# A cross-attention and routed FFN kernel: router scores spread by two transfers, normalised rows turned by VectorE and transfers, and the key projections moved to other steps

## The reference

```python
x = x + xattn(layernorm(x), ctx, ctx, mask)       # 16 heads of 16, softmax over 1024 keys
x = x + ffn(layernorm(x))
# ffn(y):
scores = y @ w_router;  _, idx = top_k(scores, 128)
x_sel  = y[idx]                                   # 128 rows, in the order of their scores
h      = rmsnorm(x_sel, g1)
x_attn = causal_self_attention(h, W_qkv) @ W_out.T
h2     = rmsnorm(x_sel + x_attn, g2)
x_ff   = (silu(h2 @ W1.T) * (h2 @ W2.T)) @ W3.T   # width DFF = 682
out    = y;  out[idx] = x_sel + x_attn + x_ff
```

## Time and profile before

| | |
|---|---|
| median of 3 runs | 889.56 us (888.82 to 891.79) |
| the profiled execution, its own time | 880.62 us |
| its span | 878.9 us |
| granted TensorE clock | 0.996 |
| PE busy | 852.3 us (97%) |
| ACT busy | 570.7 us (65%) |
| DVE busy | 312.4 us (36%) |
| POOL busy | 122.7 us (14%) |
| DMA moved | 35.58 MB, mean 40 GB/s |

### The profile page before, as it was taken

How to read it: one execution, slowest core, us unless ns; L and a number is a source line. 1 busy time by engine, 2 the same in 40 slices (tenths; PEclk the granted TensorE clock), 3 DMA queues, 4 the chain that set the end, 5 groups by cost and what they waited for, 6 DMA issues and landing times. The chain is left out here.

```text
span 878.9 us, 28281 instructions
## 1 busy us (share of the span) xinstructions
PE 852.3 (97%) x11797; PEld 297.4 (34%) x11802; DVE 312.4 (36%) x915; ACT 570.7 (65%) x648; POOL 122.7 (14%) x174
## 2 busy tenths in 40 slices
PE   7999999999999999999999999999999999999875
PEld 2322232334323433334323333233323342234343
DVE  3122245421552326421453216522274213322442
ACT  3567667676677767676677766777676766776310
POOL 4000102110120101111121101201021101200111
PEclk9999999999999999999999999999999999999999
DMA  5060101120011200211011200112002100010000
GB/s 186 14 234 3 64 17 33 54 76 11 3 37 50 80 8 27 61 32 50 8 39 50 80 8 2 37 50 80 7 5 60 32 3 7 14 49 3 7 25 11
DMA packets 27579, 35.58 MB, mean 40 GB/s; under 512 B 2083, under 2 KB 24142, under 8 KB 27448
## 3 DMA queue, kind: packets, MB, share of 16 engines
q1 hardware_dynamic: 24952, 31.73, 11.3%
q0 software_dynamic: 2496, 1.98, 1.4%
HBM read 27.53 MB, written 8.93 MB: 41 GB/s over the span
## 5 line engine op out<-in xcount | busy, mean ns | idle before, releaser
L524 ACT ACTIVATE probs<-pair_bank 128x1024 f32<-128x1024 f32 x512 | 496.4, 1021 | 222.9 <-ACTq L523 221.7
L494 PE MATMUL pair_bank<-q_sb,k_sb 32*64 32x512 f32 x4096 | 291.2, 612 | 0.4 <-PEq L492 0.3
L513 PE MATMUL o_bank<-probs,va 128*32 128x512 f32 x2048 | 274.7, 604 | 3.0 <-issue 1.5
L513 PEld LDWEIGHTS o_bank<-probs,va 128*32 128x32 f32 x2048 | 41.7, 108 | 208.2 <-issue 113.8
L494 PEld LDWEIGHTS pair_bank<-q_sb,k_sb 32*64 32x64 f32 x4096 | 62.3, 129 | 134.8 <-issue 133.5
L271 PE MATMUL m_bank<-wv_sb,ctx_in 128*32 128x256 f32 x1024 | 62.2, 380 | 0.0
L271 PE MATMUL m_bank<-ctx_in,wk_sb 128*32 128x512 f32 x480 | 61.0, 592 | 0.0
L649 DVE TENSOR_SCALAR va<-m_bank,valid 128x256 f32<-128x256 f32 x64 | 28.1, 479 | 82.8 <-DVEq L646 82.7
L605 DVE STREAM_TRANSPOSE o_blk<-o_bank 128x512 f32<-128x512 f32 x32 | 22.9, 717 | 96.4 <-DVEq L604 96.4
L271 PEld LDWEIGHTS m_bank<-wv_sb,ctx_in 128*32 128x32 f32 x1024 | 33.5, 110 | 35.9 <-issue 21.3
L271 PEld LDWEIGHTS m_bank<-hid_t,w 128*32 128x32 f32 x1392 | 39.4, 110 | 17.2 <-issue 16.3
(11 more groups left out here) (175 smaller groups left out, 627.3 us busy)
## 6 DMA issues: line engine op xcount, KB each, us to landing
ctx_in<-in_ctxT SPq DMA_DIRECT2D x7, 1024.0 KB, 4.9
x_in<-in_x SPq DMA_DIRECT2D x8, 512.0 KB, 3.9
x<-in_x SPq DMA_DIRECT2D x8, 512.0 KB, 4.3
mask_in<-in_mask SPq DMA_DIRECT2D x8, 512.0 KB, 3.9
out_dram<-base SPq DMA_DIRECT2D x8, 512.0 KB, 5.6
ctx_in<-in_ctxT SPq DMA_DIRECT2D x2, 512.0 KB, 6.9
mask_row<-in_mask SPq DMA_DIRECT2D x8, 128.0 KB, 3.9
x_tok<-in_order SPq DMA_DIRECT2D x7, 128.5 KB, 2.0
```

Source lines behind the costliest of these rows:

```text
L494: last = nc.tensor.matmul(pair_bank[pairs[r // 2]][j:j + 64, r % 2], key_tile(b, s, r)[:, j:j + 64], query_tile(b, s, r), start=True, stop ...
L513: last = nc.tensor.matmul(o_bank[32 * r:32 * r + 32], va[b % 2][:, t, HV * h:HV * h + 32], probs[s % 2][:, r], start=(t == 0), stop=(t == ...
L524: nc.scalar.activation(probs[s % 2][:, 2 * e:2 * e + 2, :], pair_bank[p][:], ACT.Exp, scale=HD ** -0.5).then_inc(s_free[p], 1)
```

## The change

1. The scores are spread without TensorE. When `score` is ready, SP stores it to `score_row` in DRAM (128 partitions of 4 values), waits for the store, and loads the row of 512 into all 128 partitions (`scores_in`). VectorE copies it, reordered, to `all_scores` ahead of `order0`. Each order stage now writes its place right behind itself. `norm0` moves from behind `order1` to behind `order0`.
2. The normalised rows are turned without TensorE. x is loaded in four transfers, one for each set of 32 partitions, so that 32x32 blocks lie ready; VectorE writes the normalised rows block by block (`blocks`), transposes the blocks (`turn`, 2 instructions of 128x512), and SP stores them by four transfers to `turned` in DRAM, waits, and loads `xn_t` (`put_blocks`). Q0 and Q1 are called R0 and R1 for it. VectorE does `stats`, `blocks` and `turn` at the end of the batch before (kind "X"), around `down`. In batch 0 they are done once behind norm0 (for batch 1) and once behind R1 (for batch 2).
3. The halves of K01 move from steps 18 and 19 to steps 7 and 8, where xT0 and xT1 stood. Steps 6, 18 and 19 of batches 1 to 6 and steps 18 and 21 of batch 0 now have no other work.
4. The last 42 columns of W2 are put behind those of W1 in the padding of the last column tile, at column 64. u1 computes both, so that w1 has two column tiles and not three. VectorE moves the 42 rows across partitions (`w_rest`) and multiplies them apart.

The FFN after the last step is unchanged but for point 4.

```diff
-           ("P", "K11:0", 4, False), ("P", "K11:1", 5, False), ("F", "spread", 6, False), ("P", "xT0", 7, False), ("P", "xT1", 8, False),
-           ("P", "Q0:0", 9, False), ("P", "Q0:1", 10, False), ("P", "V1", 11, False), ("P", "Q1:0", 12, False), ("P", "Q1:1", 13, False),
+           ("P", "K11:0", 4, False), ("P", "K11:1", 5, False), ("P", "K01:0", 7, False), ("P", "K01:1", 8, False),
+           ("P", "R0:0", 9, False), ("P", "R0:1", 10, False), ("P", "V1", 11, False), ("P", "R1:0", 12, False), ("P", "R1:1", 13, False),
...
-           ("F", "fs", FS_STEP, False), ("P", "V2", FS_STEP, False), ("P", "K01:0", 18, False), ("P", "K01:1", 19, False),
+           ("F", "fs", FS_STEP, False), ("P", "V2", FS_STEP, False),
...
-DVE_ORDER = [("A", "norm3"), ("F", "wo0"), ("F", "wo1"), ("P", "V0"), ("F", "y"), ("P", "stats"), ("P", "xn"), ("F", "order0"),
-             ("F", "order1"), ("N", "norm0"), ("F", "order2"), ("F", "order3"), ("P", "Q0"), ("P", "V1"), ("F", "selected"), ("P", "Q1"),
+DVE_ORDER = [("A", "norm3"), ("F", "wo0"), ("F", "wo1"), ("P", "V0"), ("F", "y"), ("F", "order0"),
+             ("N", "norm0"), ("F", "order1"), ("F", "order2"), ("F", "order3"), ("P", "R0"), ("P", "V1"), ("F", "selected"), ("P", "R1"),
...
-             ("N", "norm2"), ("F", "u0"), ("F", "w0"), ("F", "u1"), ("F", "w1"), ("F", "down")]
+             ("N", "norm2"), ("F", "u0"), ("F", "w0"), ("F", "u1"), ("F", "w1"), ("X", "stats"), ("X", "blocks"), ("F", "down"),
+             ("X", "turn")]
...
+        def load_x_for_blocks(sp, b):
+            sp.wait_ge(x_free, 1)
+            sp.sem_inc(x_free, -1)
+            for a in range(QT):
+                sp.dma_start(x_in[32 * a:32 * a + 32], io["x"][b, a * P:(a + 1) * P].rearrange("(t i) d -> i t d", i=32)
+                             ).then_inc(x_ready, 16)
+
+        def put_blocks(sp):
+            sp.wait_ge(blocks_ready, 1)
+            sp.sem_inc(blocks_ready, -1)
+            for a in range(QT):
+                sp.dma_start(turned[:, a * P:(a + 1) * P].rearrange("(c j) k -> j c k", j=32),
+                             blocks_t[32 * a:32 * a + 32].rearrange("j (c k) -> j c k", k=P)).then_inc(blocks_stored, 16)
+            sp.wait_ge(blocks_stored, 16 * QT)
+            sp.sem_inc(blocks_stored, -16 * QT)
+            sp.wait_ge(x_t_free, 1)
+            sp.sem_inc(x_t_free, -1)
+            sp.dma_start(xn_t[:], turned.rearrange("(c p) s -> p c s", p=P)).then_inc(x_t_ready, 16)
...
+        def spread_scores(sp):
+            sp.wait_ge(score_ready, 1)
+            sp.sem_inc(score_ready, -1)
+            sp.dma_start(score_row.rearrange("(p t) -> p t", t=QT), score[:]).then_inc(score_stored, 16)
+            sp.wait_ge(score_stored, 16)
+            sp.sem_inc(score_stored, -16)
+            sp.dma_start(scores_in[:], score_row.partition_broadcast(P)).then_inc(spread_in, 16)
...
+                if t == 0 and note is put:
+                    dve.wait_ge(spread_in, 16)
+                    dve.sem_inc(spread_in, -16)
+                    nc.vector.tensor_copy(all_scores[:].rearrange("p (t q) -> p t q", t=QT),
+                                          scores_in[:].rearrange("p (q t) -> p t q", t=QT))
...
+                if r == 1:
+                    last = nc.vector.tensor_scalar(w_rest[:], bank[i][W2_REST:W2_REST + REST, 2 * P:3 * P], 0.5, None, ALU.mult)
+                last.then_inc(bank_free[i], 1)
...
                 for b in range(B):
-                    if b + 2 < B:
-                        load_x(sp, b + 2)
+                    if b == 0:
+                        put_blocks(sp)
+                        load_x_for_blocks(sp, 2)
                     if b > 0:
+                        spread_scores(sp)
                         load_selected(sp, b - 1)
...
                     if b + 2 < B:
                         load_ctx(sp, b + 2)
+                        put_blocks(sp)
+                    if b + 3 < B:
+                        load_x_for_blocks(sp, b + 3)
```

More of the change, by code:

```diff
@@ L28 @@
 FT = 6
+REST = DFF - (FT - 1) * P
+W2_REST = 64
 BIG = 2.0 ** 30
@@ L145, in program @@
         xn_t = sb("xn_t", [P, KC, S])
+        blocks_t = sb("blocks_t", [P, QT * D])
+        turned = nc.dram_tensor("turned", [D, S], F32, kind="Internal").ap()
         o_blk = sb("o_blk", [P, S])
@@ L317, in pe_project @@
                 transposes(dst, [xn[:, t, c * P:(c + 1) * P] for t in range(QT)]).then_inc(done["xT"], 1)
-            elif stage[0] == "Q":
+            elif stage[0] in ("Q", "R"):
                 m = int(stage[1])
-                if m == 0 and part != 1:
+                if stage == "Q0" and part != 1:
                     pe.wait_ge(xT_sb, 2)
                     pe.sem_inc(xT_sb, -2)
+                elif stage == "R0" and part != 1:
+                    pe.wait_ge(x_t_ready, 16)
+                    pe.sem_inc(x_t_ready, -16)
                 dst = bank[i] if part == 1 else take_bank(pe, i)
@@ L430, in pe_ffn @@
                 dst = take_bank(pe, i)
-                for f in range(3):
+                for f in range(2 if stage == "w1" else 3):
                     last = product(dst[:, f * P:(f + 1) * P],
@@ L619, in dve_project @@
             if stage == "stats":
-                dve.wait_ge(x_ready, 16)
-                dve.sem_inc(x_ready, -16)
+                loads = 16 * (QT if b > 0 else 1)
+                dve.wait_ge(x_ready, loads)
+                dve.sem_inc(x_ready, -loads)
                 for t in range(QT):
@@ L638, in dve_project @@
                 dve.drain().then_inc(x_free, 1)
+            elif stage == "blocks":
+                dve.wait_ge(rstd_ready, 1)
+                dve.sem_inc(rstd_ready, -1)
+                by_block = xn[:].rearrange("p t d -> p (t d)").rearrange("p (c t j) -> p c t j", t=QT, j=32)
+                for t in range(QT):
+                    nc.vector.tensor_scalar(by_block[:, :, t], x_in[:, t].rearrange("p (c j) -> p c j", j=32), mv[:, t, 0:1],
+                                            rstd[:, t:t + 1], ALU.subtract, ALU.mult)
+                dve.drain().then_inc(x_free, 1)
+            elif stage == "turn":
+                flat = xn[:].rearrange("p t d -> p (t d)")
+                for half in (slice(0, S), slice(S, 2 * S)):
+                    nc.vector.transpose(blocks_t[:, half], flat[:, half])
+                dve.drain().then_inc(blocks_ready, 1)
             elif stage[0] == "V":
@@ L659, in dve_project @@
                 dve.sem_inc(done["Q"], -1)
+                if m == 1 and not general:
+                    dve.sem_inc(x_t_free, 1)
                 nc.vector.tensor_scalar(q_sb[b % 2][:, m, 0], bank[i], parity[:, 0:1], None, ALU.mult).then_inc(q_sb_ready, 1)
@@ L737, in dve_ffn @@
                 others = all_scores[:] if i == MISC else bank[i]
-                if t == 0 and i == MISC:
+                if t == 0 and note is put:
[3 more added lines that the diff above has]
+                                          scores_in[:].rearrange("p (q t) -> p t q", t=QT))
+                    dve.drain()
+                elif t == 0 and i == MISC:
                     dve.wait_ge(all_ready, 1)
@@ L751, in dve_ffn @@
                                                accum_out=rank[:, t, 1:2])
-                if t > 0:
+                if note is put:
+                    dve.drain()
+                    put(t)
+                elif t > 0:
                     note(t - 1)
-                if t == QT - 1:
+                if t == QT - 1 and note is not put:
                     dve.drain()
@@ L854, in dve_ffn @@
                 r = int(stage[1])
+                if r == 1:
+                    nc.vector.tensor_tensor(gate[0:REST, FT - 1], w_rest[:], silu2[r][0:REST, 2 * P:3 * P], ALU.mult)
                 dve.wait_ge(done["w"], 1)
                 dve.sem_inc(done["w"], -1)
[L857 to L858 removed]
+                n = 3 - r
+                nc.vector.scalar_tensor_tensor(out=gate[:, 3 * r:3 * r + n].rearrange("p f k -> p (f k)"),
+                                               in0=bank[i][:, 0:n * P], scalar=0.5, in1=silu2[r][:, 0:n * P],
+                                               op0=ALU.mult, op1=ALU.mult
                                                ).then_inc(bank_free[i], 1)
@@ L1326, in _ @@
                 for b in range(B):
-                    for stage, kind in slots(b, POOL_ORDER):
+                    for stage, kind in slots(b, POOL_ORDER if b > 0 else POOL_ORDER_0):
                         if kind == "F":
```

48 lines of the change are left out of this document (29 added, 19 removed), and 8 rows, old and new, of the table PE_SLOT_0.

## The result

| | before | changed |
|---|---|---|
| median | 889.19 us (888.12 to 891.79, 4 runs) | 883.09 us (882.56 to 883.83, 4 runs) |
| ratio, with its 95% interval | | 0.9928 (0.9905 to 0.9951) |
| the profiled execution, its own time and span | 880.62, 878.9 us | 883.09, 881.4 us |

The changed kernel is 6.1 us faster by the medians; 882.2 us was forecast. The spans of the two profiled executions must not be subtracted: that of before came from an execution some 9 us under its median, that of after from one at its median. So steps are compared, not spans.

A forecast was written before the change was run, and what follows sets the result against it. TensorE was taken as the bound, busy for 97% of the span. Terms -8.3 (middle batches), -0.24 (batch 0), +1.0 (seam) and +0.1 (batch 7) give -7.4 us: 889.56 to 882.2 us, forecast 879 to 885, wider range 876.5 to 887.

The forecast's parts named there:

- The steps of a middle batch: Batches 1 to 6: steps 6 to 8 get 0.31 us longer, steps 18 and 19 get 1.37 us shorter.
- the 0.35 us of the earlier trace: Score group behind an empty step waits 0.35 us for a PSUM pair that ScalarE's exponential gives back.
- ScalarE does not hand on its 0.35: Rival: no wait behind empty steps, each middle batch saves 1.76 + 0.44 us; 876.5 us, chance 0.1.
- The term of 1.06: Net saving of 1.06 us in each of batches 1 to 6 from steps 6 to 8, 18 and 19.
- w1: FFN product w1 with two column tiles instead of three: net 0.32 us saved a batch, bounds 0.1 and 0.44.
- Batch 0: Of batch 0's two emptied steps the first saves 0.24 us, the second nothing.
- The scores' way: Store and load of the scores through DRAM take 5.0 us, covered by VectorE's idle time before norm0; term 0.
- The rival with late transfers: Scores' store and load take over 8.0 us, norm0 is late in every batch, TensorE stands; 909 us, chance 0.07.
- The net of the batch: Batch 7: last scatter makes hid 0.4 us late, w1 saves 0.32; +0.1 us.
- The seam from batch 0 to batch 1: The turn of rows at the end of batch 0 makes norm3 late; TensorE loses 1.0 us, bounds 0 and 2.
- the gain is eaten: Rival: late down or norm3, a wait of 0.7, or w1's copy takes the gain back; 888 us, chance 0.13.
- the 8.94 us: Runs' median over the profiled execution of before; taken not to depend on the steps and carried over to the forecast.

The follow-up runs named there:

- short_exp: Changed kernel with ScalarE's exponentials over 320 of 512 queries only, so the output is not the reference's; 872.55 us, ratio 0.9808.
- turn_before_r1: Changed kernel with batch 0's stats, blocks and turn of batch 2's rows ahead of R1 in VectorE's order; 872.10 us, ratio 0.9903.
- the second set: Four runs on one chip: the changed kernel again, shorter exponentials, TensorE's spread, early turn with TensorE's spread in batch 7; 883.16, 872.55, 882.75, 882.14 us.
- w1_three_tiles: Changed kernel with point 4 undone: W2 whole, w1 with three column tiles, no w_rest; 876.29 us, ratio 0.9958.
- spread_by_pe: Changed kernel with point 1 undone: four TensorE transposes in step 6 spread the scores, ScalarE copies, no transfers; 882.75 us, ratio 0.9919.
- order3_behind_r0: Changed kernel with order3 moved behind R0 in VectorE's order; 881.41 us, ratio 1.0007.

## Why the prediction was right, point by point

**The steps of a middle batch.** Forecast 2.04, 3.25, 2.90 for steps 6 to 8 and 2.04, 2.39 for 18 and 19; found so to 0.01 us. The decisive choice was to take the 0.35 us of the earlier trace rows as a price handed to the next step. `short_exp` shows that its cause is ScalarE's exponential, and with that the rival "ScalarE does not hand on its 0.35" (876.5) falls. The term of 1.06 was right.

**w1.** 0.32 forecast, 0.37 found by undoing it. The copy of the 42 rows took 0.29 where 0.3 was taken.

**Batch 0.** By the first traces its emptied step 18 and the step behind it take 5.30 us for 5.53, 0.23 less where 0.24 was forecast, and step 21 with its follower 5.55 for 5.54, nothing, as forecast.

**The scores' way.** The two transfers' single prices were both wrong (1.4 and 4.0 for 2.0 and 2.5), and the errors partly cancelled: 5.69 us from the last score to the copy where 5.15 was taken. What made the term 0 was the slack: 1.83 us of idle were left ahead of norm0. The rival with late transfers (909) falls with it for middle batches. In batch 7 the wait did come, with 1.41 us in step 9. The net of the batch was forecast as +0.1, and by the first and last score groups it is 89.9 us against 89.8 in the first trace of before. That agreement is luck: the 89.8 has the pause of 1.54 us in step 14 that the prediction took for a wait for `hid`. The kernel before takes 89.8, 88.4 and 90.4 us for this batch in its three traces; the first and the third have the pause (1.54 and 1.81 us), the second has none. With the spread on TensorE the changed kernel takes 88.1 and 88.8, against 89.9 and 90.1 with transfers. So the transfers cost some 1.1 to 2.0 us there, more than the 0.4 that I had counted.

**The seam from batch 0 to batch 1** is the term that was mis-sized: +1.0 forecast (bounds 0 and 2), +1.77 found. norm3's transpose starts 119.94 - 115.88 = 4.06 us after the start of step 0, against 118.35 - 116.06 = 2.29 before (the earlier trace rows have the transpose; step 0 started at 116.06). I had the end of the turn right (118.95 forecast, 119.16 found), which is 0.99 of the 1.77. The other 0.78 is idle time of VectorE between turn and the transpose, at the start of a batch, for which the trace names no other engine, and which I had taken as nothing. `turn_before_r1` removes the whole.

**Sum.** Forecast -7.4; with the seam at its measured size -6.6, with w1 too -6.9. Measured were -6.1 (0.9928) and -6.6 (0.9925) with the long step 11, and about -6.7 by working out without it. A pause in step 17 (last section), 1.28 us in batch 1 of the changed kernel and 0.50 in batch 2 of before, adds some 0.8 that no term had; it is not in every kernel. The rival "the gain is eaten" (888) falls: nothing in a middle batch was given back to VectorE or SP.

**What stays open.** The forecast said that nothing shows where the 8.94 us between before's profiled execution and its runs lie, and carried them over. That held, but not for a reason that I can show, and so the nearness of 882.2 is in this part luck: the changed kernel has 9.4 us in step 11 that no term had, and they are about as much as the 8.94 carried over. On the chip where before takes 889.8 us the changed kernel loses 9.9 us in step 11; on the chips where before takes 879 to 880, its near relatives lose none there. (The changed kernel itself was not run on those.) It is plain to suppose that before loses its 9 us on that chip in the same manner. Every trace of before is from an execution near 880 us (the second and the third on chips where this is its median; the first may be from such a chip too, which is not known), so this was not seen, and it stays argued. The long step 11 also explains why the first trace after looked no shorter than that of before: its batches are 102.0 us as before's are, 1.45 of steps saved and about 1.5 lost again in step 11.

## What to carry to other kernels

Read what a step costs when it is empty, and what the step behind it then costs, before you take work out of a pipeline: here an emptied step gave 0.58 us and handed 0.35 of it on, so that two adjacent empty steps are worth more than two single ones. Hand-written orders break at their seams: the one place where the new stage stood right ahead of a releaser (norm3 at the end of batch 0) cost 1.8 us, and in the last batch the steps are shorter than those from which the cover was reckoned. A gap ahead of an instruction is not yet a wait for its operand: the earlier trace rows had a pause of TensorE itself, which a second trace of the same kernel did not have. Where the profiled execution lies far from the median, compare step by step and get a trace of both kernels on one chip before a difference of spans is believed.

## What the runs showed of the hardware

**TensorE's releases came late in all five traces with a long step 11** (that of the result, and the four of the second set, which come from one chip). In batch 2 of the changed kernel the matmuls of R0 end at about 255.2 us (the group starts at 254.16 and takes 1.04), but VectorE, idle for 2.57 us, begins R0's copy only at 256.92; in `turn_before_r1`, on another chip, the same product starts at 249.34 and the copy at 250.56. That is 2.76 us from one to the other against 1.22. ScalarE saw it too: its next pair of exponentials came 0.6 us later than in the steps around (idle 1.56 for 0.96), from the timelines of VectorE and ScalarE:

```profile
250.56 0.75 DVE L726 TENSOR_SCALAR q_sb<-m_bank,parity 128x512 f32<-128x512 f32 x1 [1.03 <-DVEq L723]
```

```profile
256.98 1.94 ACT L573 ACTIVATE probs<-pair_bank 128x1024 f32<-128x1024 f32 x2 [1.56 <-ACTq L572]
```

Two engines that wait for different semaphores of TensorE both went on late, by 1.5 and 0.6 us. The runs rule out ScalarE's pace (it stayed with short exponentials) and the spread's transfers (it stayed with the transposes), and the code alone (`turn_before_r1` and `w1_three_tiles`, with the same steps 5 to 12 in batches 1 to 6, had none of it on another chip). Each set ran on one chip at one time, so the chip and the occasion cannot be told apart. Whether POOL's scatter, issued at the same moment (at 255.26 in the changed kernel, at 250.44 in `turn_before_r1`, which had no late release), is needed for it could not be told, since it was tried only on a chip that showed no late releases.

**A pause of 1.3 us in step 17 of batch 1**, in the middle of a score group, with no wait that the trace names:

```profile
171.10 1.09 PE L543 MATMUL pair_bank<-q_sb,k_sb 32*64 32x512 f32 x9
172.41 1.08 PE L543 MATMUL pair_bank<-q_sb,k_sb 32*64 32x512 f32 x7 [0.22 <-issue]
```

The step takes 7.12 us instead of 5.84 in the changed kernel, 6.8 to 7.1 in most of its relatives, but not in `short_exp`, `spread_by_pe` or `order3_behind_r0`; in the traces of before a smaller pause of 0.5 to 0.8 us lies in the same step of batch 2. It moves with the code, costs up to 1.3 us once, and was not explained.
